# Two-layer graph network on one core: the same instructions with the places of all pieces in five queues redrawn

## What is computed

```python
# layer 0: one head of 256 columns, additive scores
h = X @ W                                     # 512 x 512 by 512 x 256
e = leaky_relu(h @ a[0] + (h @ a[1]).T, 0.2)  # masked where adj == 0
x = layernorm(X + concat([softmax(e) @ h, h]))
# layer 1: 8 heads of 64 columns
q, k, v = x @ Wq.T + bq, x @ Wk.T + bk, x @ Wv.T + bv
attn = softmax(where(adj == 0, -inf, q @ k.T / 8))
x = layernorm(x + (attn @ v) @ Wo.T + bo)
```

## Time and profile before

| | us |
|---|---|
| median of 3 runs | 3204.15 |
| lowest and highest run | 3191.07, 3204.79 |
| the profiled execution, its own time | 3193.84 |
| span of its instructions | 3192.1 |

### The profile page before, as it was taken

The page is one execution under the profiler, slowest core; times in us unless marked ns, Lnnn a source line. Parts: engine busy times, 40 slices in busy tenths (PEclk is TensorE's granted clock), DMA queues, the critical chain, the costliest instruction groups (busy, mean ns, idle before and its releaser), DMA issues.

```text
span 3192.1 us, 60592 instructions
## 1 busy us (share of the span) xinstructions
PE 2991.9 (94%) x19084; PEld 2522.3 (79%) x19084; DVE 2599.2 (81%) x6553; ACT 2462.9 (77%) x5543; POOL 2066.3 (65%) x1927
## 2 busy tenths in 40 slices
PE   5899999999999999999999999999999999999995
PEld 4788888887788887888887888887888887888874
DVE  4788888888888888888888888888888888888873
ACT  3777888777878777877878887877887778887773
POOL 1466766667666677666676666676766676666664
PEclk8999999999999999999999999999999999999997
DMA  3577877777777777777777777777777777777774
GB/s 122 171 224 212 227 227 212 218 216 222 226 217 213 217 217 225 229 215 213 218 217 227 223 225 213 217 216 228 223 225 214 215 217 229 223 221 212 212 204 143
DMA packets 290047, 681.92 MB, mean 214 GB/s; under 512 B 40512, under 2 KB 74048, under 8 KB 256960
## 3 DMA queue, kind: packets, MB, share of 16 engines
q1 hardware_dynamic: 289728, 678.05, 73.8%
...
## 4 chain that ended last, share of the span: by engine, by line
PE 41%; DMA 25%; ACT 13%; POOL 11%; SPq 4%; DVE 4%; issue 3%; ACTq 0%; DVEq 0%; POOLq 0%
PE R_bank L620 25%; DMA turned_lo_prob<-scratch 13%; POOL turned_lo_prob L1057 9%; PE O_bank L709 9%; DMA scratch<-blocked 8%; PE S_bank L690 5%; DMA r_wide<-r_scratch 4%; ACT turned_hi_prob L737 3%; SPq L522 2%; ACT prob L821 2%; DVE blocked L999 1%; ACT tokens L752 1%; PE L_bank L611 1%; ACT o_half L840 1%; POOL o_half L1052 1%
## 5 line engine op out<-in xcount | busy, mean ns | idle before, releaser
L1057 POOL TENSOR_TENSOR turned_lo_prob<-turned_lo_prob,turned_hi_prob 128x512 fp32r<-128x512 f32 x1024 | 1297.7, 1296 | 594.7 <-ACT turned_hi_prob L737 594.1
L999 DVE STREAM_TRANSPOSE blocked<-prob 128x512 f32<-128x512 f32 x1024 | 699.7, 698 | 167.7 <-ACT prob L821 128.9
L737 ACT ACTIVATE turned_hi_prob<-turned_lo_prob 128x512 fp32r<-128x512 f32 x1024 | 596.9, 622 | 300.6 <-DMA turned_lo_prob<-scratch 296.5
L821 ACT ACTIVATE prob<-prob,small_cols 128x512 f32<-128x512 f32 x1024 | 730.3, 715 | 68.7 <-DVE small_cols L979 67.0
L979 DVE CUSTOM_DVE_ANT_0 prob<-S_bank,mask 128x512 f32<-128x512 f32 x1024 | 674.3, 675 | 76.3 <-PE S_bank L690 72.8
L709 PE MATMUL O_bank<-turned_hi_prob,v_st 128*128 128x256 f32 x2048 | 526.8, 293 | 71.4 <-POOL turned_lo_prob L1057 65.9
L709 PE MATMUL O_bank<-turned_lo_prob,v_st 128*128 128x256 f32 x2048 | 509.7, 285 | 0.0
L709 PEld LDWEIGHTS O_bank<-turned_hi_prob,v_st 128*128 128x128 f32 x2048 | 394.4, 193 | 113.1 <-POOL turned_lo_prob L1057 86.9
L690 PE MATMUL S_bank<-qk_pair 64*128 64x512 f32 x3072 | 442.6, 413 | 16.1 <-DVE small_cols L979 15.0
L620 PE MATMUL R_bank<-wv,x1T 128*128 128x256 f32 x3072 | 413.9, 289 | 7.3 <-DVE qk_pair L896 5.5
L620 PEld LDWEIGHTS R_bank<-wv,x1T 128*128 128x128 f32 x3072 | 386.6, 193 | 25.2 <-issue 24.4
...
## 6 DMA issues: line engine op xcount, KB each, us to landing
scratch<-blocked SPq DMA_DIRECT2D x256, 1024.0 KB, 4.4
...
tokens<-xT SPq DMA_DIRECT2D x128, 256.0 KB, 5.9
tokens<-x SPq DMA_DIRECT2D x128, 256.0 KB, 4.2
r_wide<-r_scratch SPq DMA_DIRECT2D x512, 64.0 KB, 3.7
out<-tokens SPq DMA_DIRECT2D x128, 256.0 KB, 4.3
r_scratch<-r_cols SPq DMA_DIRECT2D x256, 2.0 KB
...
```

The costliest lines, as they stand in the source:

```text
L737: act.activation(dst, src, ACT.Copy).then_inc(done, 1)
L821: act.activation(prob_tile(R, s), prob_tile(R, s), ACT.Exp, bias=negmax[:, slot:slot + 1], scale=-1.0, accum_out=psum_row[:, ph % 2, j:j + ...
L999: dve.transpose(blocked[:, ph % 2, :, :, 2 * (s % 2) + s % 4 // 2, :].rearrange("p d c i -> p c d i"), prob_tile(R, s).rearrange("p (c d i ...
L1057: pool.tensor_tensor(turned_lo_prob[:, ph % 2, a, :, :], turned_lo_prob[:, ph % 2, a, :, :].bitcast(F32), turned_hi_prob[:, a, :, :].bitca ...
```

## The change

The tables of the five queues, `START`, `PROLOGUE` and `ENDING` are redrawn. No instruction, tile, buffer or semaphore is added or taken away, and every queue still holds the same pieces. The order of the pieces of one kind is kept. What moves is how the kinds interleave.

```diff
 TENSOR_PLAN = (
-    "scores scores E1",
-    "scores E2 V0",
+    "scores E1 scores",
+    "V0 E2 scores",
 GPSIMD_PLAN = (
-    "A0 norm",
-    "bo0 bo1",
...
-    "lo bo2",
-    "turn bo3",
+    "turn bo1",
+    "bo2 bo3",
 SP_PLAN = (
-    "sv rs",
-    "rl mv",
-    "sv fin3",
...
+    "rl sv",
+    "xt1 fin3",
+    "mv sv",
```

More of the change, by code:

```diff
@@ L56 @@
     "O0 O1 O2",
-    "C0 scores scores",
+    "scores scores C0",
     "weigh weigh O3",
@@ L60 @@
     "weigh D0 weigh",
[L61 to L64, removed]
+    "scores scores D1",
+    "W0 C2 W1",
+    "W2 A3 W3",
+    "D2 C3 weigh",
     "weigh scores scores",
@@ L79 @@
 SCALAR_PLAN = (
[L80 to L95, removed]
-    "exp evQ3 lap0 lap1",
-    "turn E0 lap2 hi",
-    "E1 hi hi exp",
-    "lows hi E2 lap3",
@@ L100 @@
[L100 to L108, removed]
+    "exp evQ1 exp N",
+    "lows turn exp exp",
+    "hi hi pre0 hi",
+    "exp exp hi aexp0",
+    "pre1 exp exp hi",
+    "hi hi lows hi",
+    "C0 exp aexp1 exp",
+    "evQ2 pre2 fin0 C1",
+    "turn fin1 fin2 lows",
+    "aexp2 hi hi evW0",
+    "pre3 C2 hi evW1",
+    "exp hi evW2 exp",
@@ L109 @@
+    "aexp3 exp evW3 C3",
+    "turn exp hi hi",
+    "hi lows exp hi",
+    "A0 exp fin3 exp",
+    "exp evQ3 lap0 lap1",
+    "lap2 E0 turn hi",
+    "hi E1 hi exp",
+    "lows hi E2 evV0",
+    "lap3 exp exp E3",
+    "turn exp evV1 hi",
+    "hi hi A1 lows",
+    "hi exp B0 exp",
+    "exp exp evQ4 turn",
+    "A2 hi hi lows",
+    "hi B1 exp exp",
+    "hi evV2 evV3 exp",
+    "B2 turn exp A3",
     "lows hi hi hi",
-    "B3 hi exp exp",
-    "turn",
+    "hi exp B3 turn",
+    "exp",
 )
 VECTOR_PLAN = (
-    "vt reduce vt reduce",
@@ L115 @@
[L115 to L131, removed]
+    "reduce vt vt reduce",
+    "vt evQ1 sum vt",
@@ L132 @@
+    "reduce reduce inv vt",
+    "vt reduce evO0 reduce",
+    "yst0 red0 evO1 inv",
+    "yst1 evO2 vt reduce",
+    "reduce yst2 vt vt",
+    "reduce evO3 reduce red1",
+    "yst3 sum C0 vt",
+    "yrs evQ2 red2 vt",
+    "evD0 C1 vt reduce",
+    "reduce lst0 evD1 reduce",
+    "sum evW0 lst1 C2",
+    "evW1 red3 evW2 vt",
+    "inv reduce evW3 vt",
+    "vt evD2 C3 vt",
+    "reduce lst2 reduce evD3",
+    "vt lst3 reduce reduce",
     "lrs sum vt vt",
@@ L134 @@
     "reduce inv E1 reduce",
-    "vt reduce E2 sum",
+    "vt sum E2 reduce",
     "vt vt E3 vt",
-    "evV0 evV1 inv reduce",
-    "reduce vt sum reduce",
-    "reduce vt B0 vt",
+    "inv evV0 evV1 reduce",
+    "reduce sum reduce vt",
+    "vt reduce B0 vt",
     "vt evQ4 inv reduce",
[L141 to L145, removed]
+    "reduce sum B1 reduce",
+    "vt reduce vt evV2",
+    "inv B2 vt evV3",
+    "sum reduce reduce vt",
+    "inv B3",
 )
@@ L153 @@
     "norm yrs",
+    "turn lo",
     "lo lo",
-    "turn lo",
     "lo norm",
```

64 lines of the change are left out of this document (33 added, 31 removed).

## The result

| | us | ratio to before, 95% interval |
|---|---|---|
| before, median of 4 runs on the same chip | 3202.16 | |
| after, median of 4 runs (3234.50 to 3241.88) | 3239.67 | 1.0122 [1.0093, 1.0150] |
| after, the profiled execution, its own time | 3234.50 | |

The change makes the kernel 1.2% slower, 37.5 us. The direction is the one predicted, and the time lies in the range, 14 us above the point.

What follows compares the result with a forecast made beforehand. The prediction took PE's queue as the bound, so only its waits could change. POOL's +21.7 us, with all other terms at 0, added to 3204.15 gave 3225.9 us; the range ran from 3190 to 3258.

Steps and rivals of the forecast that it cites:

- What bounds, and that only waits count: PE's queue bounds the kernel; reordering can win only its waits, 3.2 us idle a round, about 96 us in all.
- POOL's third `bo`: At the turn of a round, norm -1 and turn -1 come 0.70 us later, stalling O 0: 31 x 0.7 = +21.7 us.
- The sign on the page: Profile after: a hole of some 0.7 us inside O 0, 31 times; PE's R_bank row about 20 us idle, not 1.3.
- The `E` stretch: Around the E pieces PE's waits change places but stay tied to hi 16: 0 a round, ends -1.0 and +1.2.
- +0.2: On SP, mv 4 behind fin 3 goes out 0.2 us later a round, between -0.8 and +1.4.
- The slower rival: fin 3 ahead of mv 4 holds back group 4, +1 us a round on top of POOL's 0.7: 3256, chance 0.20.
- The faster rival: Waits at E fall by more than POOL costs, V 0 covering the longest: 3183, chance 0.20.
- the 0.2 of the forecast: From hi 16 to weigh 8, the new order of E pieces brings weigh 8 0.2 us sooner a round.
- Groups 6 and 7: Loops through HBM to weigh 12 and weigh -2 keep their length but for SP: 0, ends -0.4 and +0.7.
- `red` beside `lo`: VectorE's red 0, 1 and 3 beside POOL's lo: up to 1.7 us more VectorE time a round, 0 on PE, at most 0.3.
- The sum: All terms over the whole kernel: 0 + 21.7 + 0 + 0 = +21.7 us, giving 3225.9.

Runs made afterwards that it cites:

- the best kernel: The changed kernel with fin 3 and bo 1 moved back, evQ 4 one exp up, lap 3 and E 1 redrawn on ACT: 3181.72 us, ratio 0.9925.

## Why the prediction was right and where it failed

- **What bounds, and that only waits count.** Right. In the four stretches PE's idle time grew from 13.4 to 18.4 us of 400, that is 1.3 us in each 100, and the period grew by 1.4 in each 100.
- **POOL's third `bo`, +21.7.** This is the term that was mis-sized. Alone in the kernel before, it gave 0.79 us of wait and +17 to +19 us. In the change it gave +0.31 us a round at `O` 0, the very low end, some 9 us, and the times don't tell it from nothing. The step that failed is the sentence that both ends hang on `lo` 31 so that nothing earlier heals it. PE did not hang on `lo` 31 any more: `weigh` -2 waits 0.11 in place of 0.53, since the rest of the round delivers group 7 earlier relative to PE: `lo` 31 starts 2.08 us into the round, 2.72 before. That is what the third `bo` adds to POOL's chain, so `norm` -1 starts at the same time as before (7.73 and 7.72), and the hole is the 0.31 us by which PE begins `O` 0 sooner (7.40 against 7.71). A delay added behind a wait that the same change shortens is paid out of that wait.
- **The sign on the page.** The wait was put on PE's row, about 20 us in place of 1.3. PE's row has 2.8, the 16.1 us stand on the row of the weight loads, and PE's busy time in its row grew by 8.5 us (371.9 to 380.4). With the 1.5 us more of idle time that is 10 us, 31 x 0.31: most of the hole is counted as busy there. With the term at full size it is 12.0 on PE's list and 0.79 each on PEld. A wait ahead of a matmul inside a piece is to be looked for on both.
- **The `E` stretch, 0.** Right for PE's order, wrong in sum. PE's order alone changes nothing measurable (0.9990 [0.9978, 1.0001]), `hi` 16 to `weigh` 8 was forecast at 6.4 against 6.59 and came at 6.57 (table, before 6.69). What failed is the start of this chain: `mv` 4 was taken at +0.2 and measured +0.37, and `hi` 16, which should have followed at the same distance, came +0.87. From the issue of `mv` 4 to `hi` 16 it took 0.5 us longer, with 256 KB of `fin` 3 just ahead; 0.2 of it is left when `fin` 3 goes out early.
- **What +0.2 left out.** The working had all that was needed: `fin` 3 ready 1.1 us after `sv` 4 has landed. It then took most of that back, since things ahead of it move up. They did, but `sv` 4 moved up with them (0.37 us at its issue, 0.78 at its landing), and with it the time from which `mv` 4 could go. What moves both ends of a wait does not shorten it by as much. The measured gap between the landed store and `mv` 4 is 1.16 us, where the old times give 1.4 (1688.2 against 1686.73). So against the round's start `mv` 4 is only 0.37 us late, near the forecast, but 0.94 later than the new order gives it with `fin` 3 out of the way (52.92 against 51.98).
- **The slower rival.** It is what happened: `fin` 3 costs 41 us in the change, where the rival had 30. It was priced as coming on top of POOL's 0.7, and it decides from `fin` 3 being ready later than `sv` 4 lands, which held. Its mechanism deserved the forecast's place. Its time, 3256, lies about as far from the measured one as the forecast's.
- **The faster rival.** Right in that the stretch had a gain to give: with `fin` 3 out of the way E 0 to `weigh` 8 is 0.67 us a round shorter than before, between its 0 and -1.0. It was hidden under the slower one. But its reason, V 0 as cover, isn't what the runs show: PE's order alone gave nothing. Of the 0.67, 0.44 is `hi` 16 starting sooner behind E 0 (3.01 us against 3.45), and 0.23 the way from `hi` 16 to `weigh` 8 (6.46 against 6.69), the 0.2 of the forecast.
- **Groups 6 and 7, 0 with ends -0.4 and +0.7.** +0.59, inside. The prediction looked at SP. By the table it is the place of `hi` 27 on ACT that holds `weigh` 12, and the edit that moves it takes this delay away in the best kernel. In the change itself that is worked out, not run.
- **`red` beside `lo`, 0 on PE.** Right as far as a trace shows it. Line L924 after, against 648/685/1258:

```profile
L924 DVE CUSTOM_DVE_ANT_0 alpha<-alpha,mask x128: 657/1108/1785, 37.9 to 3054.9; 128x512 f32<-128x512 f32 x128
```

  In the mean of a round `red` 0, 1 and 3 take 1.32, 1.15 and 1.28 us, and together 1.7 us a round above 0.69 each, the most that was forecast, and VectorE is busy 38 us longer in all. The longest is 1.10 us above the median of before, where 0.57 each was taken. None of PE's waits names it. By the Trainium skill, SBUF — State Buffer, section SBUF: two separate sides, a VectorE instruction with two SBUF inputs and a GpSimd instruction that reads SBUF lock each other out, so that the one that starts second waits for the other to end. The trace agrees, with a loss on both engines: `lo` 3, 7 and 11, which stand beside these `red`, take 1.5 to 1.7 us where the others take 1.30. No run took the overlap away alone, so that it costs PE nothing is argued, not shown.
- **The sum.** 21.7 forecast, 37.5 measured. That the time lies in the range is luck in part, since the forecast's one term isn't what made it: in its place stand about 36 us from the `E` stretch (31 x 1.16), 18 from groups 5 and 6, and -13 from the first part of the round, 41 by the two profiled executions.
